# A two-layer post-norm decoder: norms' inverse roots by one power on GpSimd, half-width query projections, probability rings of six

## The reference, cut to what matters

```
x = ln(x + self_attention_0(x))        # 16 heads of 8, rotary, causal
x = ln(x + cross_attention_0(x, ctx))  # one head of 128, 1601 context rows of 96
x = ln(x + experts_0(x))               # 32 experts of 64 and a shared one, top 8
x = ln(x + self_attention_1(x))        # 16 heads of 8, relative positions, causal
x = ln(x + cross_attention_1(x, ctx))  # 12 heads of 64, 1601 context rows, padding mask
x = ln(x + experts_1(x))               # two experts, width 128
def layernorm(x): return (x - mean(x)) / sqrt(var(x) + 1e-5)
```

## Time and profile before

| | |
|---|---|
| median of 3 runs | 2157.14 us (2140.36 to 2173.19) |
| the profiled execution, its own time | 2159.29 us |
| its span from first to last instruction | 2157.5 us |
| PE busy | 1857.2 us (86%), 19672 matmuls |
| POOL busy | 1100.0 us (51%) |
| DVE busy | 1189.9 us (55%) |
| ACT busy | 903.4 us (42%) |
| mean granted TensorE clock | 0.906 of full |

### The profile page before, as it was taken

The page is one execution under the profiler, slowest core; times in us unless marked ns, Lnnn a source line. Parts: engine busy times, 40 slices in busy tenths (PEclk is TensorE's granted clock), DMA queues, the critical chain, the costliest instruction groups (busy, mean ns, idle before and its releaser), DMA issues.

```text
span 2157.5 us, 50937 instructions
## 1 busy us (share of the span) xinstructions
PE 1857.2 (86%) x19672; PEld 1395.8 (65%) x19672; DVE 1189.9 (55%) x3159; ACT 903.4 (42%) x1875; POOL 1100.0 (51%) x1664
## 2 busy tenths in 40 slices
PE   5666889898898988889898988989888998989996
PEld 3443467576676666666675776756666666767775
DVE  5253447554665546744575546744477545754552
ACT  2522344444443444345343444434443453434443
POOL 2502363557535573356635674354743566356664
PEclk9975689899998998988998999988999899999998
DMA  6000010001000010000100010000000000000000
GB/s 173 26 1 1 1 26 1 1 2 27 4 2 2 2 27 4 1 3 4 27 2 2 2 27 4 2 3 2 27 4 1 2 2 4 2 1 2 2 4 3
DMA packets 24146, 23.30 MB, mean 11 GB/s; under 512 B 16266, under 2 KB 22132, under 8 KB 23412
## 3 DMA queue, kind: packets, MB, share of 16 engines
q1 hardware_dynamic: 23892, 19.89, 3.4%
HBM read 18.83 MB, written 1.05 MB: 9 GB/s over the span
## 4 chain that ended last, share of the span: by engine, by line
PE 44%; POOL 22%; issue 16%; DVE 12%; ACT 4%; POOLq 0%; SPq 0%; DMA 0%; DVEq 0%; ACTq 0%
POOL xp_l L1444 9%; POOL pr_l L1444 6%; PE ps L934 4%; PE ps L936 3%; PE ps L935 3%; PE ps L901 3%; PE ps L1112 3%; PE ps L952 3%; PE ps L953 3%; PE ps L954 3%; PE ps L896 2%; DVE smax L1730 2%; DVE xmax_x L1808 1%; PE ps L1097 1%; PE ps L1099 1%
## 5 line engine op out<-in xcount | busy, mean ns | idle before, releaser
L1444 POOL TENSOR_TENSOR xp_l<-xp 128x512 f16<-128x512 f32 (+1 forms) x672 | 665.4, 993 | 761.9 <-ACT xp L1292 754.0
L1292 ACT ACTIVATE xp<-ps 128x512 f32<-128x512 f32 (+1 forms) x672 | 380.2, 566 | 564.4 <-PE ps L936 472.1
L1808 DVE TENSOR_REDUCE xmax_x<-ps 128x1 f32<-128x512 f32 x576 | 391.9, 687 | 350.4 <-PE ps L901 342.2
L1444 POOL TENSOR_TENSOR pr_l<-pr 128x512 f16<-128x512 f32 (+1 forms) x248 | 249.5, 1030 | 131.4 <-ACT pr L1244 119.7
L952 PE MATMUL ps<-c_tok,xp 128*128 128x97 f16 (+1 forms) x1248 | 202.9, 215 | 11.5 <-POOL xp_l L1444 5.8
L952 PE MATMUL ps<-cx_tok,xp 128*128 128x97 f16 (+1 forms) x1248 | 198.1, 212 | 11.6 <-ACT oq L1302 6.1
L953 PE MATMUL ps<-c_tok,xp 128*128 128x97 f16 (+1 forms) x1248 | 201.8, 214 | 0.0
L954 PE MATMUL ps<-c_tok,xp_l 128*128 128x97 f16 (+1 forms) x1248 | 201.7, 213 | 0.0
L953 PE MATMUL ps<-cx_tok,xp 128*128 128x97 f16 (+1 forms) x1248 | 197.1, 211 | 0.0
L954 PE MATMUL ps<-cx_tok,xp_l 128*128 128x97 f16 (+1 forms) x1248 | 197.0, 211 | 0.0
L936 PE MATMUL ps<-xq_h,c_hl 96*128 96x256 f16 (+1 forms) x624 | 181.3, 291 | 0.0
(11 more groups left out here) (367 smaller groups left out, 4541.6 us busy)
## 6 DMA issues: line engine op xcount, KB each, us to landing
ct<-in_ctxT SPq DMA_DIRECT2D x8, 600.4 KB
raw_tok<-in_ctx SPq DMA_DIRECT2D x8, 576.0 KB
c_wg<-in_wg SPq DMA_DIRECT2D x1, 1088.0 KB, 7.7
c_wu<-in_wu SPq DMA_DIRECT2D x1, 1088.0 KB, 9.8
c_wd<-in_wd SPq DMA_DIRECT2D x1, 1088.0 KB, 4.9
xin<-in_x SPq DMA_DIRECT2D x8, 128.0 KB, 2.1
out<-ys SPq DMA_DIRECT2D x8, 128.0 KB, 1.9
c_wd<-in_sel SPq DMA_DIRECT2D x1, 768.0 KB
```

The source lines that it names most:

```text
L1292: fn(xp_slot(i, n)[0:k_, 0:w], bank(first_bank + n % 2, k_, 0, w), ACT.Exp, scale=scale).then_inc(xa_e[i].sem, 1)
L1444: sub = lambda out, a, b_: nc.gpsimd.tensor_tensor(out, a, b_, ALU.subtract)
L1808: red(cross.xmax[:, t, c:c + 1], bank(PART_BANK[q], P, 0, PARTS[c][1]), AX.X, ALU.max).then_inc(xa_xd[1].sem, 1)
```

## The change

It does three things. **The norm:** DVE adds epsilon and writes minus the mean to a new tile `nm`; POOL raises variance plus epsilon to the power -0.5 in one instruction with two tensors (`fixed` now holds -0.5) and multiplies by minus the mean; the 14 operations become two, both in one piece. The number of pieces stays six. **The projections:** while the weights are folded, DVE splits the folded query weights into float16 high and low parts (three new operations on 128x1188 elements, the low part times 64). ACT writes the transposed tokens as a float16 high part and again divided by 64 (two operations in place of one), DVE subtracts the high part for a low one (`tokens_low`), and `project` is three half-width products. PE waits for `xl_ready`, set by DVE, where it waited for ACT's copy. **The rings:** `pr` and `pr_l` have six places, and the value products come one pair later in self attention and one step later in cross attention 0; what is left then stands at the end.

```diff
-STEPS = (73, 82, 206, 30, 21)
+STEPS = (67, 74, 182, 26, 17)
+RING = 6
+LOW = 64.0
-        pr = sb("pr", [P, 4, 2 * SEQ])
+        pr = sb("pr", [P, RING, 2 * SEQ])
-        pr_l = sb("pr_l", [P, 4, 2 * SEQ], F16)
+        pr_l = sb("pr_l", [P, RING, 2 * SEQ], F16)
 ...
 # PE, self_attention
                 for g in range(0, 12, 2):
                     scores((g, g + 1))
-                    if g:
-                        values(g - 2)
-                        values(g - 1)
-                    yield
-                values(10)
+                    if g > 2:
+                        values(g - 4)
+                        values(g - 3)
+                    yield
+                for g in range(8, 11):
+                    values(g)
                 m = values(11)
 # PE, context_attention
-                    if p >= 2:
-                        values(p - 2)
-                    yield
-                values(NPAIR - 2)
-                values(NPAIR - 1)
+                    if p >= 3:
+                        values(p - 3)
+                    yield
+                for p in range(NPAIR - 3, NPAIR):
+                    values(p)
 # PE, project
-                mm(bank(4, KE, 0, SEQ), a_mat[:, 1 + h, :], cross.xt[:, 1:1 + SEQ], start=True, stop=True, skip_group_check=True).then_inc(xa_q[1].sem, 1)
+                o = bank(4, KE, 0, SEQ)
+                mm(o, am_h[:, h, :], xq_in[:, 0, :], start=True, stop=False, skip_group_check=True)
+                mm(o, am_l[:, h, :], xq_in[:, 1, :], start=False, stop=False, skip_group_check=True)
+                mm(o, am_h[:, h, :], xq_in[:, 2, :], start=False, stop=True, skip_group_check=True).then_inc(xa_q[1].sem, 1)
 # PE, cross_start and cross_steps (step p == 5 of head 9)
-                                    pe.wait_ge(xt_ready[4].sem, xt_ready[4].at(b.plus(1), 1))
+                                    pe.wait_ge(xl_ready.sem, xl_ready.at(b.plus(1), 1))
 # ACT, stream
+                if n == 4:
+                    nc.scalar.copy(xq_in[:, 0, :], bank(4, P, 0, SEQ))
+                    fn(xq_in[:, 1, :], bank(4, P, 0, SEQ), ACT.Copy, scale=1.0 / LOW).then_inc(xt_ready[4].sem, 1)
 # POOL, rounds
-                for last in (False, False, True):
-                    then(g.tensor_tensor(q, y, y, ALU.mult))
-                    then(g.tensor_tensor(q, q, var, ALU.mult))
-                    then(g.tensor_tensor(q, q, fixed[:, 0, :], ALU.add))
-                    then(g.tensor_tensor(y, y, q, ALU.mult))
-                    if last:
-                        then(g.tensor_tensor(q, side.mv[:, :, 0], y, ALU.mult))
-                        then(g.tensor_tensor(q, q, fixed[:, 1, :], ALU.mult))
-                    yield
-                yield
-                yield
+                then(g.tensor_tensor(y, var, fixed[:], ALU.pow))
+                then(g.tensor_tensor(q, side.nm[:], y, ALU.mult))
+                for _ in range(NORM - 1):
+                    yield
 # DVE, folding
+                step(v.tensor_copy(am_h[:], a_mat[:, 1:, :]))
+                settle()
+                step(tt(a_mat[:, 1:, :], a_mat[:, 1:, :], am_h[:], ALU.subtract))
+                settle()
+                ts(am_l[:], a_mat[:, 1:, :], LOW, None, ALU.mult).then_inc(unfolded, 1)
 # DVE, normalise
-                step(ts(side.nr[:, 0, :], side.mv[:, :, 1], EPS, None, ALU.add))
-                settle()
-                step(ts(side.nri[:], side.nr[:, 0, :].bitcast(I32), -0.5, float(0x5F3759DF), ALU.mult, ALU.add))
-                settle()
-                ts(side.nr[:, 0, :], side.nr[:, 0, :], -0.5, None, ALU.mult).then_inc(nv[n].sem, 1)
+                ts(side.nr[:, 0, :], side.mv[:, :, 1], EPS, None, ALU.add)
+                ts(side.nm[:], side.mv[:, :, 0], -1.0, None, ALU.mult).then_inc(nv[n].sem, 1)
 # DVE, new; called in cross_start and, before the reduction at p == 5 of head 9, in cross_steps
+            def tokens_low(b):
+
+                dve.wait_ge(xt_ready[4].sem, xt_ready[4].at(b, 1))
+                tt(xq_in[:, 2, :], bank(4, P, 0, SEQ), xq_in[:, 0, :], ALU.subtract).then_inc(xl_ready.sem, 1)
```

More of the change, by code:

```diff
@@ L276, in decoder_kernel @@
         a_c = sb("a_c", [KE, 1 + XH])
+        am_h = sb("am_h", [P, XH, KE], F16)
+        am_l = sb("am_l", [P, XH, KE], F16)
+        xq_in = sb("xq_in", [P, 3, SEQ], F16)
         g_mat = sb("g_mat", [DC + 1, 1 + XH, D + 1])
@@ L291, in __init__ @@
             def __init__(self, c):
-                self.xt = sb("xt" + c, [P, 1 + SEQ])
+                self.xt = sb("xt" + c, [P, 1 + SEQ]) if c == "_f" else None
                 self.res = [sb(f"res{n}{c}", [P, QT, D]) for n in range(1 if c == "_f" else 2)]
@@ L297, in __init__ @@
                 self.nri = sb("nri" + c, [P, QT], I32)
+                self.nm = sb("nm" + c, [P, QT])
                 self.xmax = sb("xmax" + c, [P, QT, 4])
@@ L304, in decoder_kernel @@
         carrier = sb("carrier", [P, 1])
-        fixed = sb("fixed", [P, 2, QT])
+        fixed = sb("fixed", [P, QT])
         qk_h = sb("qk_h", [P, 2, SEQ], F16)
@@ L388, in xp_slot @@
         def xp_slot(i, n):
-            return xp[:, n % 3, :] if i == 1 else pr[:, n % 4, :]
+            return xp[:, n % 3, :] if i == 1 else pr[:, n % RING, :]
         def pr_high(g):
-            return pr[:, g % 4, :].bitcast(BF16)[:, 1::2]
+            return pr[:, g % RING, :].bitcast(BF16)[:, 1::2]
         def xp_high(n, k_, c0, w):
@@ L416, in decoder_kernel @@
         nv = [count(f"nv{n}") for n in range(7)]
-        nw = [count(f"nw{n}", 14) for n in range(7)]
+        nw = [count(f"nw{n}", 2) for n in range(7)]
         def both(name, per):
@@ L441, in decoder_kernel @@
         sa_u = both("sa_u", 1)
+        xl_ready = count("xl_ready")
         sa_on = both("sa_on", 1)
@@ L655, in folding @@
                     yield
-                pe.wait_ge(unfolded, 2 * (1 + XH) + XH + 2)
+                pe.wait_ge(unfolded, 2 * (1 + XH) + XH + 3)
                 yield
@@ L795, in values @@
                             o, q0 = bank(5, P, (t * NH + h) * (HD + 1), HD + 1), k * n + (t - kt) * P
-                            high, low = pr_high(g)[:, q0:q0 + P], pr_l[:, g % 4, q0:q0 + P]
+                            high, low = pr_high(g)[:, q0:q0 + P], pr_l[:, g % RING, q0:q0 + P]
                             mm(o, high, v_h[:, kt, h, :], start=(g == 0 and k == 0 and t == 0), stop=False, skip_group_check=True)
@@ L861, in values @@
                         mm(o, c.tok_l[0:k_, kt, :], pr_high(p)[0:k_, cols], start=False, stop=False, skip_group_check=True)
-                        m = mm(o, c.tok_h[0:k_, kt, :], pr_l[0:k_, p % 4, cols], start=False, stop=(kt == NK - 1), skip_group_check=True)
+                        m = mm(o, c.tok_h[0:k_, kt, :], pr_l[0:k_, p % RING, cols], start=False, stop=(kt == NK - 1), skip_group_check=True)
                     if p == NPAIR - 1:
@@ L1008, in cross_start @@
                 yield
-                pe.wait_ge(xt_ready[4].sem, xt_ready[4].at(b, 1))
+                pe.wait_ge(xl_ready.sem, xl_ready.at(b, 1))
                 for h in range(3):
@@ L1183, in stream @@
                 act.wait_ge(tr_ready[n].sem, tr_ready[n].at(b, 1))
-                side, bk = (cross, 4) if n == 4 else (front, 5)
-                nc.scalar.copy(side.xt[:, 1:1 + SEQ], bank(bk, P, 0, SEQ)).then_inc(xt_ready[n].sem, 1)
+                if n == 4:
+                    nc.scalar.copy(xq_in[:, 0, :], bank(4, P, 0, SEQ))
+                    fn(xq_in[:, 1, :], bank(4, P, 0, SEQ), ACT.Copy, scale=1.0 / LOW).then_inc(xt_ready[4].sem, 1)
+                else:
+                    nc.scalar.copy(front.xt[:, 1:1 + SEQ], bank(5, P, 0, SEQ)).then_inc(xt_ready[n].sem, 1)
             def normalise(b, n, side, res):
@@ L1196, in normalise @@
                     act.wait_ge(x_out.sem, b.n * 16 + 16)
-                act.wait_ge(nw[n].sem, nw[n].at(b, 14))
+                act.wait_ge(nw[n].sem, nw[n].at(b, 2))
                 y = side.nri[:].bitcast(F32)
@@ L1243, in self_attention @@
                     act.wait_ge(sa_s[i].sem, sa_s[i].at(b, g + 1))
-                    fn(pr[:, g % 4, :], bank(6 + g % 2), ACT.Exp, scale=SA_SCALE).then_inc(sa_e[i].sem, 1)
+                    fn(pr[:, g % RING, :], bank(6 + g % 2), ACT.Exp, scale=SA_SCALE).then_inc(sa_e[i].sem, 1)
                     if g % 2:
@@ L1457, in then @@
                     done += 1
-                    if done < 14:
+                    if done < 2:
                         pool.wait_ge(nw[n].sem, nw[n].at(b, done))
@@ L1484, in attention_low @@
                     pool.wait_ge(sa_e[i].sem, sa_e[i].at(b, g + 1))
-                    sub(pr_l[:, g % 4, :], pr[:, g % 4, :], pr_high(g)).then_inc(sa_l[i].sem, 1)
+                    sub(pr_l[:, g % RING, :], pr[:, g % RING, :], pr_high(g)).then_inc(sa_l[i].sem, 1)
                     if g % 2:
@@ L1526, in context_attention @@
                     pool.wait_ge(xa_e[0].sem, xa_e[0].at(b, p + 1))
```

(11 more changed lines are left out.)

## The result

The changed kernel takes 2070.7 us (median of four runs, 2070.3 to 2072.7) where before takes 2159.9 beside it (2140.4 to 2173.2): ratio 0.963, 95% interval 0.959 to 0.966. The direction and most places were right; the sum was too small, 56 us against 89 between the two profiled executions (2159.3 and 2070.3).

The account below looks back on a forecast made before the run. PE, busy 86% of the span, bounds the kernel by its work and waits; 19.2 + 3.4 + 10.4 + 5 + 19 + 11 - 1.5 - 10.5 = 56 us off 2159.3 is 2103, forecast 2104 us, range 2075 to 2145.

Parts of the forecast that it names:

- folding: Three new DVE operations on 128x1188 when the query weights are folded: 1.5 us lost, ends nothing and 4.7.
- join: At head 9, PE newly waits for DVE's subtraction behind four reductions: 1.75 us in each of six, 10.5 us lost.
- The norm alone with nothing beside it: Four norms at the start, two at the end: each gains 3.2 us, 19.2 us in all.
- The norm behind the experts: The one loop norm of six that leaves PE idle: 1.73 us gained, six times, 10.4 us.
- The other five gain nothing: The loop's other five norms of six: no gain, as PE does not wait at their transposes.
- the stream term: Norm rounds in front of stream subtractions go: 5 us gained, half of PE's 11.2 us wait; ends none and all.
- the 9 for cross attention 0: Value products behind GpSimd's low parts in cross attention 0: 9 of 11.3 us of PE's waiting gained.
- The rings: Value products later in self attentions and cross attention 0: 19 us gained in all, ends 8 and 31.8.
- The projections: 96 query projections, 0.15 us shorter each, 14.4 us; three quarters reach the time, 11 us, ends 5 and 19.
- Rival 1: Stalls move on to GpSimd and DVE in dense phases, new pauses may lower the clock: 2140 us, chance 0.35.
- rival 3: More comes back: 2.4 GHz where waits go, rings and projections at upper ends; 27 us more, 2077 us, chance 0.12.

Follow-up runs that it names:

- kernel 1: The kernel before with the new norm alone; measured 2105.5 us, ratio 0.974.
- the two sets: Four runs, then six more, of the changed kernel with DVE's new subtraction at head 9 one step earlier: 2057.0 us, then 2052.6 us.
- the version with the join earlier: The changed kernel with DVE's new subtraction at head 9 put ahead of four row-maximum reductions: 2057.0 us, then 2052.6 us.

## Why the prediction was right, and where it was too small

The 89 us lie at three places: 24.3 at the start, 9.4 at the end, 55.6 in the loop, of which 36.8 is waiting and work and 18.7 is clock. The prediction's terms put 15.7, 6.4 and 33.9 there. Its mechanism held. Of the missing 33 us, 19 are a clock gain for which the sum had no term, as far as one execution of each kernel shows it; the rest is the norm, priced some 17 us too low, less the projections with folding and join, which cost 5 alone where the sum had 1.

- **The norm alone with nothing beside it** held: 3.1 us at the first norm, 7.07 to 3.94 at the last transposes, 8.12 to 5.00 ahead of the last scaling.
- **The norm behind the experts** was priced too high, 1.73 us a time. This is that place now, and the row of ACT in the trace of before that the prediction did not use:

```profile
601.89 0.87 ACT L1214 ACTIVATE xsf<-res_f,nr_f,nri_f 128x128 f32<-128x128 f32 x2
...
602.82 0.44 PE L673 MATMUL ps<-c_ident,xsf 128*128 128x128 f32 x2 [0.93 <-ACT xsf L1214]
```

```profile
634.78 0.88 ACT L1200 ACTIVATE xsf<-res_f,nr_f,nri_f 128x128 f32<-128x128 f32 x2 [0.85 <-POOL nr_f L1472]
```

  Of PE's 1.73 us only the 0.85 in which ACT itself waited for POOL could go; the other 0.9 is ACT's scaling. 4.8 us in six, not 10.4.
- **"The other five gain nothing"** failed, and with it half of the stream term. PE does not wait at their transposes, but the product behind one of them waited for ACT's copy, which stood behind another norm's scaling (router, 5.1 us), and of the rounds that stood in front of stream subtractions I took half where all but 0.6 of 11.2 us went. The step that failed is the reading of a norm's price at its transposes alone: a chain that is 3 us shorter also frees what its engine did next. Norm in all, by kernel 1 less the clock: 18.9 + 27.7 + 8.9 = 55.5 us, where 38 was forecast (and a part of the 9 for cross attention 0).
- **The rings**: 19 forecast, 5.4 + 13.3 = 18.7 alone. Right in sum, with more at the start (1 was taken). In self attention 0 the waits moved to the last pair, as forecast, two waits of 0.48 and 0.54 us:

```profile
1194.89 2.03 POOL L1458 TENSOR_TENSOR pr_l<-pr 128x512 f16<-128x512 f32 x2
```

```profile
1195.98 0.18 PE L804 MATMUL ps<-vm,pr 128*128 128x9 f16 x1 [0.48 <-POOL pr_l L1458]
...
1196.98 0.18 PE L804 MATMUL ps<-vm,pr 128*128 128x9 f16 x1 [0.54 <-POOL pr_l L1458]
```

  In cross attention 0 the first pair waits 0.34 us where it was 1.26, with the power and its product directly ahead of the subtractions:

```profile
1229.21 0.69 POOL L1479 TENSOR_TENSOR nri_x<-nr_x,fixed 128x2 f32<-128x2 f32 x1
1229.98 0.20 POOL L1480 TENSOR_TENSOR nr_x<-nm_x,nri_x 128x2 f32<-128x2 f32 x1
1230.13 4.03 POOL L1458 TENSOR_TENSOR pr_l<-pr 128x512 f16<-128x512 f32 x4
...
1231.22 0.32 PE L868 MATMUL ps<-pr,cx_tok 128*97 128x256 bf16 x1 [0.34 <-POOL pr_l L1458]
```

- **The projections** were priced too low in time, 0.33 to 0.42 us. They take 0.46 from start to start (and 0.42 at the least):

```profile
519.74 0.31 PE L905 MATMUL ps<-xq_in,am_h 128*99 128x256 f16 x1
519.89 0.27 PE L906 MATMUL ps<-xq_in,am_l 128*99 128x256 f16 x1
520.00 0.27 PE L907 MATMUL ps<-xq_in,am_h 128*99 128x256 f16 x1
520.20 0.27 PE L926 MATMUL ps<-ident,xneg_x 128*1 128x128 f16 x2
```

  The first of the three and the product behind the last each cost some 0.04 to 0.09 more than the 0.11 of a row in sequence. Of the 0.06 to 0.10 us each, next to nothing reached the end: with the join's wait gone, the loop less the clock is 1495.5 us with the projections and 1497.4 without. 11 was forecast.
- **The join**: 10.5 charged, 10.2 measured by taking it away. That is the wait itself; some 2 us of it came back at the score group ahead, and the time fell by 14 and 18 us in the two sets.
- **The clock.** Rival 1 said that the join's pause may bring 1.2 GHz with it, and rival 3 that 2.4 GHz returns where waits go. Each came true in one kernel: the projections alone lost 31 us by it, the changed kernel gained 19. The join alone does not decide, since both wait 12.2 us there; but it has a part, as rival 1 said. With it gone, the clock's cost fell from 133 to some 108 us in the projections alone, and in the changed kernel it stayed (84 and 87). Rival 3's time, 2077, was the nearest, though neither the rings nor the projections were at their upper ends. What sets the 1.2 GHz stretches in one order of the work and not in another stays open; the runs show only that they are not a sum over the parts.

## What to carry to other kernels

Price a shorter chain at every engine that it passes, not only at the wait that names it, and read the waiting engine's own releaser first: what lies behind it in series does not go. When a part is tried alone and a few per cent decide, hold the granted clock beside the time, and first see that it is on record for the whole stretch: here one part lost 30 us alone and was worth 25 in company, and by the split the clock was most of the one and more than all of the other. A new wait is cheapest mended by order: look whether its work can stand ahead of what the waiting engine also needs.

## What the runs showed of the hardware

- A power of two tensors of 128x2 takes 0.69 us on GpSimd, 3.5 times the 0.20 of a multiplication of that shape, the first one as every other.
- The clock's cost in the loop, for nearly the same matmuls, lay between 84 and 133 us, so that norm and rings and the version with the join earlier differ by 32 us in their profiled executions (2093.8 and 2061.4), but in the loop less the clock by 2.
- A 128x2 operation of DVE that takes 0.17 us took 0.49 in a norm beside GpSimd's subtractions, by the row below. In the changed kernel this operation (line 1677) took 0.17 us in all 20 norms in which GpSimd was idle when it began, and 0.42 to 0.97 in 27 of the 28 in which GpSimd was busy. The Trainium skill (Advanced Engine Details and Errata, VectorE Performance Modes) says that GpSimd and VectorE's two-port modes share a port and block each other; the trace agrees with that, 0.49 against 0.17. Why the next operation of the same shape (line 1678) took 0.16 in 47 of 48 stays open.

```profile
499.19 0.49 DVE L1677 TENSOR_SCALAR nr_x<-mv_x 128x2 f32<-128x2 f32 x1
```
